# Per-batch weight scales of a mixture of experts against one scale for all experts, found during the convolution

## What is computed

```
t = _to_tokens(x)                                    # x + the weighted copies
t = t + _L0_ffn_ref(_ln_t(t), Wr, br, W1, b1, W2, b2, gamma, beta)
# _L0_ffn_ref, for tokens x:
logits = jnp.mean(x, axis=1) @ Wr + br               # one row per image: 4 x 8
...
top_w, top_i = jax.lax.top_k(rw_tok, K)              # K = 2 of 8 experts per image
h = jax.nn.gelu(jnp.einsum('nd,edf->enf', xf, W1) + b1[:, None, :], approximate=False)
y = jnp.einsum('enf,efd->end', h, W2) + b2[:, None, :]
...
out = _layer_norm(out + x, gamma, beta)
```

## Time and profile before

| | us |
|---|---|
| median of 3 runs | 1072.17 (1070.05 to 1075.75) |
| profiled execution, its own time | 1070.16 |
| its span, first to last instruction | 1068.4 |
| PE busy | 970.3 (91%) |
| DVE busy | 731.8 (68%) |
| ACT busy | 541.4 (51%) |
| TensorE's granted clock, mean | 0.956 |

### The profile page before, as it was taken

One profiled execution on the slowest core, in us unless ns is written; L12 is line 12 of the kernel. 1 busy time (PEld: TensorE's weight loads), 2 busy tenths in 40 slices (PEclk: granted clock), 3 DMA queues, 4 the chain that ended last, 5 costly groups with the idle time before them and its releaser, 6 DMA issues. The chain is left out here.

```text
span 1068.4 us, 19438 instructions
## 1 busy us (share of the span) xinstructions
PE 970.3 (91%) x7649; PEld 749.9 (70%) x7649; DVE 731.8 (68%) x1826; ACT 541.4 (51%) x963; POOL 144.3 (14%) x163
## 2 busy tenths in 40 slices
PE   2675899999999999999999835999999999999997
PEld 1565666677677666667999833777787777777776
DVE  3656545648845953655766746689888987998776
ACT  5556243344443522234455325857667685676751
POOL 1000000000010002110112201011111121112211
PEclk9878899999999999999999866999999999999999
DMA  9411111101400201022555442052133214212101
GB/s 267 146 38 44 45 45 45 50 19 52 123 23 2 81 27 52 14 46 46 164 156 172 113 131 66 3 147 60 32 85 95 61 43 135 61 31 61 42 19 45
DMA packets 89692, 77.08 MB, mean 72 GB/s; under 512 B 24604, under 2 KB 86445, under 8 KB 89502
## 3 DMA queue, kind: packets, MB, share of 16 engines
q1 hardware_dynamic: 79680, 66.32, 22.3%
q10 hardware_dynamic: 9920, 9.51, 2.9%
HBM read 46.42 MB, written 29.40 MB: 71 GB/s over the span
## 5 line engine op out<-in xcount | busy, mean ns | idle before, releaser
L1213 PE MATMUL pM<-V,U 128*128 128x368 f16 (+3 forms) x2016 | 319.4, 314 | 0.0
L1213 PEld LDWEIGHTS pM<-V,U 128*128 128x128 f16 x2016 | 194.3, 97 | 100.6
L1702 ACT ACTIVATE gf<-pH,b1c,sc 128x384 f32<-128x384 f32 x192 | 127.9, 669 | 110.0 <-issue 89.8
L1896 DVE SCALAR_TENSOR_TENSOR gl<-gf,sc,gh 128x384 f16<-128x384 f32 x192 | 146.1, 792 | 43.6 <-ACT gh L1693 43.0
L2053 PE MATMUL pY<-w2h,gh 128*128 128x256 f16 x576 | 157.0, 273 | 0.0
L2053 PE MATMUL pY<-w2l,gh 128*128 128x256 f16 x576 | 157.0, 273 | 0.0
L2053 PE MATMUL pY<-w2h,gl 128*128 128x256 f16 x576 | 157.0, 273 | 0.0
L2037 PE MATMUL pH<-xh,w1h 128*128 128x384 f16 x384 | 127.0, 331 | 6.2 <-DVE w1l L1855 5.5
L2037 PE MATMUL pH<-xl,w1h 128*128 128x384 f16 x384 | 126.8, 330 | 0.0
L2037 PE MATMUL pH<-xh,w1l 128*128 128x384 f16 x384 | 126.8, 330 | 0.0
L696 ACT CAST V<-pV 128x384 f16<-128x384 f32 x96 | 45.5, 477 | 153.7 <-PE pV L1184 153.6
(11 more groups left out here) (260 smaller groups left out, 1490.5 us busy)
## 6 DMA issues: line engine op xcount, KB each, us to landing
xa<-in_xt SPq DMA_DIRECT2D x16, 576.0 KB, 6.2
xs_scratch<-xs SPq DMA_DIRECT2D x16, 576.0 KB, 4.3
tk<-t_scratch SPq DMA_DIRECT2D x24, 384.0 KB, 3.4
out<-o SPq DMA_DIRECT2D x24, 384.0 KB, 2.7
U<-xs_scratch SPq DMA_DIRECT2D x16, 480.0 KB, 4.5
w1r<-in_ew SPq DMA_DIRECT2D x8, 512.0 KB, 4.1
w2r<-in_ew SPq DMA_DIRECT2D x8, 512.0 KB, 6.2
V<-in_w1g SPq DMA_DIRECT2D x5, 784.0 KB, 14.6
```

What stands on the lines that cost most here:

```text
L1213: return nc.tensor.matmul(out[:, :, first:end], U[:, k, hi_u, piece, :], V[:, b % 2, hi_v, k, c, :, first + TILES * d:end + TILES * d], st ...
L1702: nc.scalar.activation(gf[:, (JB * m + j) % GBUFS, :], pH[:, (JB * m + j) % HBUFS, 0:CN], ACT.Gelu, bias=b1c[:, j // FB, j % FB:j % FB + 1 ...
L1896: stt(gl[:, sl, j, :], gf[:, (JB * m + j) % GBUFS, :], scale_of(b, G_UP), gh[:, sl, j, :], ALU.mult, ALU.subtract).then_inc(g_step, 1)
```

## The change

In the convolution's fourth batch SP loads the first and second weights and the biases of all eight experts, in 19 units (18 of 512 KB in SBUF, one small) through three places in `xs1`, and DVE takes the largest absolute value of each, three units behind each product k = 2 to 7 and one behind k = 8. Each load after the third waits for the unit three before it, and the loads stand ahead of `load_back` on SP. One matmul of PE in the weighted sums adds them over the partitions. The second block then makes ten scales once, on DVE ahead of the router (`scales`), and all batches use them; `largest_w1`, `largest_w2`, `bound`, `scales_1` and `scales_2` go. `turn_stats` of the last batch moves ahead of `sum_tokens`. `bet` and `gam` are loaded ahead of the experts, b2 behind w2. ACT normalises the first chunk before the last exponential of the router, and chunk 1 is turned and taken before layer 1 of chunk 0. The first batch's w2h is made by DVE, and Gelu of chunk 0 waits for b1 alone.

```diff
+EXPERTS = 8
+B2_UNITS = 2
+UNITS_1, UNITS = EXPERTS + 1, 2 * EXPERTS + 1 + B2_UNITS
+STAGES, UNITS_SLOT = 3, 3
+SUMS_AT = 448
...
+        stage = [xs_all[:, k * 4 * C * 2:(k + 1) * 4 * C * 2].bitcast(F32) for k in range(STAGES)]
...
+            e, w = (u, ew1) if u < EXPERTS else (u - UNITS_1, ew2)
+            return w[e].rearrange("(f p) c -> p f c", p=P), here.rearrange("p (f c) -> p f c", f=w.shape[1] // P)
...
+            sp.wait_ge(v_turned, V_TURNS * IMGS)
+            for u in range(UNITS):
+                if u >= STAGES:
+                    sp.wait_ge(unit_taken, u - STAGES + 1)
+                src, dst = unit(u)
+                sp.dma_start(dst, src).then_inc(unit_loaded[u % STAGES], 16)
...
+            def take_unit(u):
+                dve.wait_ge(unit_loaded[u % STAGES], 16 * (u // STAGES + 1))
+                nc.vector.tensor_reduce(largest[:, u:u + 1], unit(u)[1] if u == EXPERTS else stage[u % STAGES],
+                                        AX.XY if u == EXPERTS else AX.X, ALU.max, apply_absolute_value=True).then_inc(unit_taken, 1)
...
+                        for u in range(UNITS_SLOT * (k - 2), min(UNITS_SLOT * (k - 1), UNITS)) if k >= 2 else ():
+                            take_unit(u)
...
+            dve.wait_ge(units_summed, 1)
+            nc.vector.tensor_copy(wsum[:, :], pC[:, SUMS_AT:SUMS_AT + UNITS]).then_inc(wsum_taken, 1)
...
+                if n == IMGS - 2:
+                    pe.wait_ge(unit_taken, UNITS)
+                    nc.tensor.matmul(pC[:, SUMS_AT:SUMS_AT + UNITS], ones[:, :], largest[:, :],
+                                     start=True, stop=True).then_inc(units_summed, 1)
...
             sum_added(B - 1)
+            turn_stats(B - 1)
             sum_tokens(IMGS - 1)
             sum_shifts(B - 1)
-            turn_stats(B - 1)
...
-SC1_STEPS, SC_STEPS = 8, 15
+V1, HB, V2, W1_UP, G_UP, W2_UP, W1_DOWN, Y_DOWN, B2_UP, NSC = range(10)
+SC_STEPS = 11
...
                 for k, e in enumerate(chosen):
-                    sp.dma_start(b1r[:, k], ew_b(eb1, e)).then_inc(b_loaded, 16)
-                    sp.dma_start(b2r[:, k], eb2[ds(e, 1), :].broadcast_to([P, C])).then_inc(b_loaded, 16)
+                    sp.dma_start(b1r[:, k], ew_b(eb1, e)).then_inc(b1_loaded, 16)
                 for k, e in enumerate(chosen):
                     sp.dma_start(w2r[:, k], ew2[ds(e, 1)].rearrange("e (f p) c -> p (e f) c", p=P)
                                  ).then_inc(w2_loaded, 16)
+                for k, e in enumerate(chosen):
+                    sp.dma_start(b2r[:, k], eb2[ds(e, 1), :].broadcast_to([P, C])).then_inc(b2_loaded, 16)
 
             def ew_b(eb1, e):
                 return eb1[ds(e, 1)].rearrange("e p f -> (e p) f")
 
             for m in range(2):
                 load_chunk(0, m)
+            sp.dma_start(bet[:, :], beta.broadcast_to([P, C])).then_inc(gb_loaded, 16)
+            sp.dma_start(gam[:, :], gamma.broadcast_to([P, C])).then_inc(gb_loaded, 16)
             sp.wait_ge(r_step, 16)
             load_experts(0)
-            sp.dma_start(bet[:, :], beta.broadcast_to([P, C])).then_inc(gb_loaded, 16)
-            sp.dma_start(gam[:, :], gamma.broadcast_to([P, C])).then_inc(gb_loaded, 16)
             for m in range(2, AHEAD):
...
-            for k in range(3):
-                act.wait_ge(r_step, (2, 11, 17)[k])
-                if k < 2:
-                    nc.scalar.activation(r[:, 2 * k + 1, :], r[:, 2 * k, :], ACT.Exp).then_inc(r_exp, 1)
-                else:
-                    nc.scalar.activation(rc[:, 5:6], rc[:, 4:5], ACT.Exp).then_inc(r_exp, 1)
-                    nc.scalar.activation(rc[:, 7:8], rc[:, 4:5], ACT.Gelu)
-
...
+            for k in range(2):
+                act.wait_ge(r_step, (2, 11)[k])
+                nc.scalar.activation(r[:, 2 * k + 1, :], r[:, 2 * k, :], ACT.Exp).then_inc(r_exp, 1)
             normalise(0, 0)
+            act.wait_ge(r_step, 17)
+            nc.scalar.activation(rc[:, 5:6], rc[:, 4:5], ACT.Exp).then_inc(r_exp, 1)
+            nc.scalar.activation(rc[:, 7:8], rc[:, 4:5], ACT.Gelu)
+            take_x(0, 0)
             normalise(0, 1)
-            take_x(0, 0)
+            take_x(0, 1)
             split_w1(0)
-            act.wait_ge(bias_step, 3)
+            act.wait_ge(bias_step, 1)
             gelus(0, 0)
-            take_x(0, 1)
-            act.wait_ge(r_step, R_STEPS + 1)
-            split_w2(0)
             normalise(0, 2)
 
...
+            def scales():
...
+                s.did(nc.vector.reciprocal(scale_of(W1_UP, 3), scale_of(V1, 3)))
+                s.did(nc.vector.tensor_scalar(scale_of(W1_DOWN), scale_of(V1), 1.0 / X_SCALE, None, ALU.mult))
+                s.did(tt(scale_of(Y_DOWN), scale_of(V2), scale_of(HB), ALU.mult))
+                s.settle()
+                s.did(nc.vector.tensor_scalar(scale_of(B2_UP), scale_of(W2_UP), scale_of(G_UP), 1.0 / B2_TOP,
+                                              ALU.mult, ALU.mult))
+                s.at(SC_STEPS)
...
+            scales()
             dve.wait_ge(r_pe, 1)
-            softmax_shift(pT[0:B, 1, 0:EXPERTS], r[:, 0, :], 0)
+            softmax_shift(pY[0:B, 0, 0:EXPERTS], r[:, 0, :], 0)
...
             s.at(R_STEPS)
+            take_x(0, 0)
             dve.wait_ge(r_pe, 3)
-            nc.vector.tensor_copy(wbc[:, :], pT[:, 1, 64:64 + TOPK * B]).then_inc(r_step, 1)
+            nc.vector.tensor_copy(wbc[:, :], pY[:, 2, 0:TOPK * B]).then_inc(r_step, 1)
             dve.wait_ge(r_step, R_STEPS + 1)
...
-            def largest(dst, src):
-                return nc.vector.tensor_reduce(dst, src, AX.X, ALU.max, apply_absolute_value=True)
-
-            def largest_w1(b):
-                if not is_first(b):
-                    dve.wait_ge(bound_ready, 2 * b - 1)
-                for k in range(TOPK):
-                    dve.wait_ge(w1_loaded[k], 16 * (b + 1))
-                    largest(mxs[:, 0, k:k + 1], w1r[:, k].rearrange("p c f -> p (c f)")).then_inc(max_step, 1)
-                dve.wait_ge(b_loaded, 64 * (b + 1))
-                largest(mxs[:, 0, TOPK:TOPK + 1], b1r[:, :, :].rearrange("p k f -> p (k f)")).then_inc(max_step, 1)
-
-            def largest_w2(b):
...
-            def powers(s, b, at, n, down):
...
-            def scales_1(b):
...
-            def scales_2(b):
...
+            dve.wait_ge(sc_step, SC_STEPS)
+            nc.vector.tensor_scalar(wvs[:, :], wbc[:, :], scale_of(W2_UP), None, ALU.mult).then_inc(sc_step, 1)
+            dve.wait_ge(sc_step, SC_STEPS + 1)
 
             def split_w1(b):
 
+                s = Steps(dve, bias_step, b, 3)
                 for k in range(TOPK):
                     dve.wait_ge(w1hi_ready, TOPK * b + k + 1)
-                    stt(w1l[:, k], w1r[:, k], scale_of(b, W1_UP), w1h[:, k], ALU.mult, ALU.subtract).then_inc(w1_step, 1)
-                s = Steps(dve, bias_step, b, 3)
-                dve.wait_ge(b_loaded, 64 * (b + 1))
-                if not is_first(b):
-                    dve.wait_ge(gelu_done, JB * CHUNKS * b)
-                s.did(nc.vector.tensor_copy(b1c[:, :, :], b1r[:, :, :]))
+                    stt(w1l[:, k], w1r[:, k], scale_of(W1_UP), w1h[:, k], ALU.mult, ALU.subtract).then_inc(w1_step, 1)
+                    if k == 0:
+                        dve.wait_ge(b1_loaded, 32 * (b + 1))
+                        after(dve, gelu_done, JB * CHUNKS * b)
+                        s.did(nc.vector.tensor_copy(b1c[:, :, :], b1r[:, :, :]))
+                dve.wait_ge(b2_loaded, 32 * (b + 1))
                 s.did(nc.vector.tensor_scalar(b2c[:, 0, :], b2r[:, 0, :], wbc[:, ds(TOPK * b, 1)], None,
...
+            def split_w2(b, high=False):
                 for k in range(TOPK):
+                    if high:
+                        dve.wait_ge(w2_loaded, 32 * (b + 1))
+                        nc.vector.tensor_scalar(w2h[:, k], w2r[:, k], wvs[:, ds(TOPK * b + k, 1)], None,
+                                                ALU.mult).then_inc(w2hi_ready, 1)
...
             half = JB // 2
-            take_x(0, 0)
-            largest_w1(0)
-            scales_1(0)
+            take_x(0, 1)
             split_w1(0)
             split_hidden(0, 0, range(JB))
-            take_x(0, 1)
-            largest_w2(0)
-            scales_2(0)
-            split_w2(0)
+            split_w2(0, high=True)
             split_b2(0)
 
             def body(b):
...
-                    if m == CHUNKS - 3 and later(b, m, 3, CHUNKS):
-                        scales_1(b + 1)
-                    if m == CHUNKS - 2 and later(b, m, 2, CHUNKS):
-                        scales_2(b + 1)
...
-                    if m == CHUNKS - 4 and later(b, m, 4, CHUNKS):
-                        largest_w1(b + 1)
-                    if m == CHUNKS - 3 and later(b, m, 3, CHUNKS):
-                        largest_w2(b + 1)
...
-            pe.wait_ge(r_step, R_STEPS)
-            nc.tensor.matmul(pT[:, 1, 64:64 + TOPK * B], ones[0:B, :],
 ```

(18 more changed lines are left out.)

150 lines of the change are left out of this document (62 added, 88 removed).

## The result

| | us | against before |
|---|---|---|
| before, median in this comparison | 1071.45 | |
| after, median | 1081.63 (1079.27 to 1082.78) | 1.0079 [1.0049, 1.0109] |
| after, profiled execution | 1081.44, span 1079.6 | span of before 1068.4 |
| forecast | 1058 (1051 to 1066) | faster |

The forecast was wrong, in sign too. Three marks divide the two spans. The first is the first matmul of the tail's attention, right behind the fourth batch's convolution: 502.75 before, 531.19 after, so **28.4 us lost** up to there (1.3 of them are no loss: one and the same load of an image goes out at 351.15 after and at 349.85 before, ahead of everything that the change touches). The second is POOL's first instruction of the second block: 626.35 and 655.19, so the tail between the two takes 123.6 and 124.0.

What follows compares the result with a forecast made beforehand. PE was taken as full from 672 on and in the convolution's fourth batch, but waiting for largest values at the change of block. 6.0 - 1.3 - 14.4 - 2.7 = -12.4 from 1070.16 gave 1057.8, said as 1058 (1051 to 1066).

Steps and rivals of the forecast that it cites:

- Part 1: Convolution's fourth batch: DVE's added reductions and the unit loads make PE wait at three places, a cost of +6.0 us.
- the clock falls: Rival: in the convolution, matmuls after PE's wait run at half speed, costing 1.5 to 2 us; within the forecast's 0.66.
- Part 2: End of the first block: `turn_stats` runs earlier, so the last statistics land before DVE's last step, -1.3 us.
- Part 3: Start of the second block: layer 2 of chunk 0 starts at +35.0 instead of +49.4, a gain of -14.4 us.
- each milestone: Second block, from its start: w1's loads at +7.7, layer 1 +15.7, first Gelu +17.7, layer 2 +35.0 us.
- +49.4: Second block of the kernel before: start of layer 2 of chunk 0, in us counted from the block's start at 626.25.
- Part 4: Later batches of the second block: six pairs of `bound` matmuls and the waits for them go, -2.7 us.
- The loads starve DVE: Rival in the convolution: slow unit loads, 1060 to 1065, chance 0.12; from 3.5 us a load 1070 to 1080, 0.05.

Runs made afterwards that it cites:

- E1: The kernel after with the one load of G (113 partitions) issued as two, of 112 partitions and of 1: 1061.48 us.
- E12: E9 with `turn_stats` behind `sum_tokens` and `sum_shifts` again, as in the kernel before: 1053.94 us.
- E9: E5 with images 0 and 1 loaded ahead of unit 15 and image 2 ahead of unit 18, instead of all four behind the last unit: 1056.91 us.
- E11: E9 with beta and gamma loaded behind the experts again, instead of ahead of them: 1053.08 us.
- E5: The kernel after with G as 112 and 1 partitions, maps' loads as 48 and 1 rows, first units asked for earlier, reductions over eleven products: 1059.05 us.

## Why the prediction was wrong, point by point

- **Part 1, the failed step.** It said that a load "lands 4.1 us after its issue", and used this for every unit, the first included. For sixteen of them it was near (3.6 to 6.3), for the first three it was 31.6, 21.4 and 18.9. The forecast never asked what was queued ahead of the unit loads on SP; it priced only the transfers' own rate. What the runs showed in its place is DVE standing 17.6 us in front of the first unit and TensorE 14.6 behind DVE, 20.2 us of time with the lower clock that followed (after against E1). The forecast had 6.0 for all of part 1; the first mark moved by 28.4 - 1.3 = 27.1. The row was there: the first of the earlier trace rows has a DMA share of 0.05 at 22 GB/s from 427.4 to 444.9, a transfer that crawls on one engine, until 441.7, through the place into which the units were to go. I read its DVE columns and passed over its last two.
- **Part 1, the rest.** With G in two (E1) its three waits came: for the low parts of the maps 1.2 (forecast 1.5), at the first spread items 3.4 (3.8), at product 8 1.9, which is 1.4 more than before (1.5). E1's first block is 7.9 longer than before's up to the second mark, against 6.0 - 1.3 = 4.7: 1.3 of it precede the change, and 21 matmuls behind the 3.4 us wait took 5.84 instead of 3.34. That is the rival *the clock falls*, priced at 1.5 to 2, and it belonged into the sum.
- **Part 2** was right in mechanism and about right in size: 1.0 to 1.4, forecast 1.3 (E12 against E9, and before against after). In the spans of before and after it is hidden by the scatter of the tail, 123.6 and 124.0.
- **Part 3** was right in size: 14.6 for 14.4, each milestone within 0.4. Its +49.4 for before was 0.2 too much (675.50 is +49.2). One reason in it was wrong: w1l is quick because it comes before `tb` could, not because of the order of the loads (E11).
- **Part 4** was right: 17.6 - 14.6 = 3.0, for 2.7.
- **The rivals.** *The loads starve DVE* had the sign, the place ("DVE stands in `take_unit`") and the time (1070 to 1080) nearly, but its mechanism was a rate of 150 GB/s for all loads, and its chance rested on 301 GB/s measured elsewhere. What came was one transfer in front. A rate measured where a queue is clear says nothing of a place where it isn't.

Had G been in two, the measured time would have been E1's 1061.48: 3.5 above the forecast of 1058, and inside its range.

## What to carry to other kernels

Before you put loads into a stretch, read the DMA share and the rate of that stretch, and ask of each transfer that is in flight there how many of the 16 DMA engines it uses: a share near 1/16 that lasts is a slow transfer, hidden only as long as nothing is queued behind it. Here the remedy was to split 113 partitions into 112 and 1. The maps' loads on 49 rows show seven marks of transfer each and gained nothing from their split: both are there 8.1 us after the first issue whole (after) and 8.3 in parts (E5). A reduction that is hidden on its own engine still has two further prices: the wait for its data in front of the engine's other work, and whatever the loading queue holds back until it is done: in E5 that was four images and, behind them, 8 KB of constants for which TensorE stood 4.2 us.
